# Last attention of an eleven-stage kernel: the largest scores subtracted in quarters of TensorE's rows, once a step

## The reference

```python
xq, xk, xv = jnp.split(hidden_states @ qkv_w.T + qkv_b, ...)   # 16 query heads, 4 key/value heads, D = 64
xq = xq * (1.442695041 / 8 * softplus(scaling))
scores = jnp.einsum('bqhd,bkhd->bhqk', xq, repeat(xk, 4))
probs = jax.nn.softmax(scores, axis=-1)
out = jnp.einsum('bhqk,bkhd->bqhd', probs, repeat(xv, 4))
return out.reshape(B, S, H * D) @ o_w.T + o_b
```

## Time and profile before

| | us |
|---|---|
| median of 3 runs | 2960.47 |
| lowest, highest | 2956.91, 2961.09 |
| the profiled execution | 2955.35 |
| its span, first to last instruction | 2953.2 |
| TensorE busy | 2582.3 |
| DVE busy | 2001.4 |
| ACT busy | 1426.9 |
| POOL busy | 1199.8 |

### The profile page before, as it was taken

How to read it: one execution, slowest core, us unless ns; L and a number is a source line. 1 busy time by engine, 2 the same in 40 slices (tenths; PEclk the granted TensorE clock), 3 DMA queues, 4 the chain that set the end, 5 groups by cost and what they waited for, 6 DMA issues and landing times.

```text
span 2953.2 us, 40282 instructions
## 1 busy us (share of the span) xinstructions
PE 2582.3 (87%) x15225; PEld 1239.7 (42%) x15230; DVE 2001.4 (68%) x3126; ACT 1426.9 (48%) x2454; POOL 1199.8 (41%) x677
## 2 busy tenths in 40 slices
PE   6679995897666997799868999999999999999898
PEld 4423333444223776477732333333333333333344
DVE  7676666404886775477567888778887888788502
ACT  5455552313543775377633555545554555455421
POOL 1135550000694554255411555545554555455300
PEclk9699997898787999899989999999999999999999
DMA  5000001001001000000000000000000000000000
GB/s 193 1 1 1 1 1 44 1 0 40 0 0 54 1 1 1 1 1 2 16 0 1 9 9 8 9 8 9 9 9 8 9 9 8 9 9 9 4 0 15
DMA packets 20685, 37.40 MB, mean 13 GB/s; under 512 B 10446, under 2 KB 12622, under 8 KB 19468
## 3 DMA queue, kind: packets, MB, share of 16 engines
q1 hardware_dynamic: 20492, 34.83, 3.4%
HBM read 32.47 MB, written 2.35 MB: 12 GB/s over the span
## 4 chain that ended last, share of the span: by engine, by line
PE 55%; DVE 27%; POOL 7%; issue 6%; ACT 4%; DMA 0%; ACTq 0%; DVEq 0%; POOLq 0%; SPq 0%
PE PS L2342 12%; PE PS L2333 11%; PE PS L1147 7%; DVE NR L2549 5%; PE PS L2303 4%; POOL WK L1551 4%; POOL WK L1904 4%; DVE WK L1854 2%; DVE W L2567 2%; DVE WK L808 2%; PE PS L1133 2%; ACT WK L767 1%; DVE WK L1870 1%; DVE WK L1864 1%; PE PS L2289 1%
## 5 line engine op out<-in xcount | busy, mean ns | idle before, releaser
L2549 DVE TENSOR_REDUCE NR<-PS 128x2 f32<-128x1024 f32 x512 | 626.3, 1223 | 208.4 <-PE PS L2304 208.3
L2444 ACT ACTIVATE WK<-PS 128x1024 f32<-128x1024 f32 x512 | 497.0, 1022 | 488.9 <-PE PS L2333 416.2
L2619 POOL TENSOR_TENSOR W<-W,WK 128x1024 f32<-128x1024 f32 x224 | 527.1, 2353 | 478.9 <-DVE W L2567 410.5
L2342 PE MATMUL PS<-WK,W 128*64 128x512 f32 x2048 | 494.1, 603 | 0.0
L2333 PE MATMUL PS<-WK 64*128 64x512 f16 (+1 forms) x4096 | 485.2, 377 | 0.0
L2567 DVE TENSOR_TENSOR W<-W,WK 128x1024 f32<-128x1024 f32 x224 | 284.8, 1272 | 14.7 <-ACT WK L2444 14.3
L2333 PEld LDWEIGHTS PS<-WK 64*128 64x128 f16 (+1 forms) x4096 | 199.2, 94 | 219.9 <-ACT WK L2444 6.5
L868 POOL TENSOR_TENSOR WK<-WK 128x512 f32<-128x512 f32 x128 | 166.1, 1298 | 178.1 <-ACT WK L761 178.1
L2303 PE MATMUL PS<-WK 64*128 64x512 f16 x512 | 196.5, 384 | 37.2 <-DVE NR L2549 35.0
L2342 PEld LDWEIGHTS PS<-WK,W 128*64 128x64 f32 x2048 | 124.0, 136 | 249.3 <-issue 174.3
L1147 PE MATMUL PS<-WK,W 128*128 128x512 f32 x512 | 220.1, 592 | 0.0
(11 more groups left out here) (362 smaller groups left out, 4660.7 us busy)
## 6 DMA issues: line engine op xcount, KB each, us to landing
XB<-l_rdens SPq DMA_DIRECT2D x62, 128.0 KB, 2.9
W<-in_mw SPq DMA_DIRECT2D x8, 512.0 KB, 12.1
W<-in_l2w SPq DMA_DIRECT2D x1, 3114.0 KB, 10.2
W<-in_f1w SPq DMA_DIRECT2D x1, 2816.0 KB, 18.8
W<-in_l3w SPq DMA_DIRECT2D x1, 2816.0 KB, 9.6
W<-in_f3w SPq DMA_DIRECT2D x1, 2816.0 KB, 11.2
W<-in_mw SPq DMA_DIRECT2D x8, 256.0 KB, 12.0
CBB<-in_cbb SPq DMA_DIRECT2D x1, 1360.0 KB, 8.4
```

The lines of the kernel that those rows point to most:

```text
L2342: m = e.matmul(k.PS[64 * i:64 * i + 64, 4, :], self.V[:, kt, g, :], self.PTB[kt // 2 % 2][:, kt % 2, i, :], start=kt == 0, stop=kt == NT - 1)
L2444: e.activation(self.PTB[kt // 2 % 2][:, kt % 2, :, :], self.k.PS[:, 2 * (kt % 2):2 * (kt % 2) + 2, :], ACT.Exp, scale=1.0 / 64).then_inc(s ...
L2549: e.tensor_reduce(self.PM[ji % 2][:, u // 4, :, u % 4], self.k.PS[:, 6:8, :], AX.X, ALU.max).then_inc(self.maxes.sem)
L2619: e.tensor_tensor(ac, ac, p, ALU.add).then_inc(self.acc1.sem)
```

## The change

The fourth part leaves the loop of scores. A new function, `pe_shift`, does it for both tiles of the step at once: four matmuls, each on a quarter of the rows (32 rows of `part`, now 1/32, by 32 rows of `MX`), into banks 0, 1, 2 and 3. It stands behind the first maxima of the step. Both tiles raise `score` there, one on the second and one on the fourth of these matmuls.

```diff
                 self.pe_max(e, j0, u0)
+                self.pe_shift(e, ji)
                 if g == self.PROJECT and ji + 2 < 32:
...
-        parts = ((self.KH[:, g, s_], qh), (self.KL[:, g, s_], qh), (self.KH[:, g, s_], ql), (self.part, mx))
+        parts = ((self.KH[:, g, s_], qh), (self.KL[:, g, s_], qh), (self.KH[:, g, s_], ql))
         for j, (keys, queries) in enumerate(parts):
             for i in range(2):
                 own = slice(64 * i, 64 * i + 64)
-                m = e.matmul(k.bank(2 * (kt % 2) + i), keys[own, :], queries[own, :], start=j == 0, stop=j == 3)
-        m.then_inc(self.score.sem)
+                e.matmul(k.bank(2 * (kt % 2) + i), keys[own, :], queries[own, :], start=j == 0, stop=False)
+
+    def pe_shift(self, e, ji):
+
+
+        for a in range(2):
+            for i in range(2):
+                rows = slice(64 * i + 32 * a, 64 * i + 32 * a + 32)
+                m = e.matmul(self.k.bank(2 * a + i), self.part[rows, :], self.MX[ji % 2][rows, :], start=False, stop=True)
+            m.then_inc(self.score.sem)
...
-        e.memset(self.part, 1.0 / 64).then_inc(self.const_part.sem)
+        e.memset(self.part, 1.0 / 32).then_inc(self.const_part.sem)
```

More of the change, by code:

```diff
@@ L2322, in pe_scores @@
         s_, n = slice(kt * 128, (kt + 1) * 128), 16 * ji + kt
-        qh, ql, mx = self.QH[ji % 3], self.QL[ji % 3], self.MX[ji % 2]
+        qh, ql = self.QH[ji % 3], self.QL[ji % 3]
         if not kt:
```

## The result

The changed kernel takes 2973.2 us (median of 5 runs, 2970.82 to 2974.71) against 2960.47 (2954.8 to 2961.09): the ratio is 1.0052, 95% interval 1.0041 to 1.0063. The forecast was 2976, slower by 0.55%. The profiled execution took 2971.78 us (2971.5 had been worked out for it); its span is 2969.7, 16.5 above before. The medians moved by 12.7 us and not by the 16 of the forecast.

The account below looks back on a forecast made before the run. TensorE was taken to bound the kernel (1094 of 1117 us busy), with DVE close behind. Terms 16.7 - 1.2 + 0.7 gave +16 us, so 2976 us on the median, 0.55% slower; range 2953 to 2994.

Parts of the forecast that it names:

- M1 to M0: Plain step, second maxima (M1) to first maxima (M0): 1.96 to 1.72 us; 0.24 saved, 0.19 becomes waiting for DVE.
- M0 to the weighing: Plain step, first maxima to weighing: 0.31 us to the added four matmuls, then 0.32 to the weighing, including shape changes.
- The weighing: Plain step, weighing and the second maxima behind it: stays at 1.88 us, with DVE's 3.98 us loop still covered.
- 185 plain steps: Six of eight steps in 30 full jobs, plus 5 steps of job 30: 0.09 us longer each, +16.7 us.
- Steps 5 and 6: Two steps of each job already set by DVE, at 4.28 and 4.59 us: no change.
- Steps without maxima: The 11 steps with no DVE wait: 3.70 to 3.59 us each, -1.2 us in all.
- The end: Last step, scores' start to DVE's sum: 3.14 to 3.85 us because exponentials start later, +0.7 us.
- Rival A: Entering the quarters costs nothing: plain step 4.13 us, total 2956.5, almost all within 0.2%; chance 0.22.
- B: The four matmuls run as two successive pairs, +0.22 us a step: about +68, 3028 us; chance 0.08.
- C: First maxima do not wait for DVE: step 4.04 us, -19, 2941 us; chance 0.10 including free entry with part of this.

Follow-up runs that it names:

- halved reductions: DVE reduces 256 of 512 columns of each bank: 2895.46 us (ratio 0.9795) in the changed kernel, 2919.11 us (ratio 0.988) in the kernel before.
- the first experiment: Changed kernel with the four quarter matmuls in front of the first maxima instead of behind: 2957.08 us against 2956.74 for the kernel before, ratio 1.0002.
- the halves: Changed kernel with the fourth part on 64-row halves again, as two pairs, still behind the first maxima: 2993.71 us, ratio 1.0124.
- the second pack: Changed kernel with the four quarter matmuls issued twice in a row, with 1/64, same result: 3020.84 us, ratio 1.0217.

## Why the prediction was right

Term by term, by its own steps:

1. *M1 to M0, 1.96 to 1.72.* Measured 1.953 to 1.716. The halved reductions show the cause: 0.195 of the 0.43 saved had turned into the wait.
2. *M0 to the weighing, 0.31 and 0.32.* Measured 0.322 and 0.324. This was the open term, since no row of before had a 32-row operand behind a 64-row one. The change costs 0.095 (the first experiment) or 0.096 (against the halves), as at the 8-row matmul of the earlier trace rows. The hundredth missed is the 0.01 of fill behind a pair that had waited, which the prologue's row had in its 0.32; with halved reductions, where M0 does not wait, M0 to the four is 0.312. The Trainium skill, page "TensorEngine Tiling (Array Packing)", section Tiling Modes, says that a change of the tiling mode drains TensorE; the runs agree that it costs time, 0.095 us from 64 to 32 rows, and do not show how. The prediction had worked out 0.1 us a step more from the figure of 3.07 times in the Trainium skill, page "TensorE: Matmul & The Clock Gate", section Part 3: Packing small matmuls. Inside this stream no run shows that: the second pack adds 0.216.
3. *The weighing, 1.88.* Measured 1.870; DVE's loop stayed below it.
4. *185 plain steps by 0.09, 16.7 us.* Measured 0.100 in the median step. Added up over the stage the six positions became 18.1 us longer, steps 5 and 6 1.0 shorter and the last steps 1.0 shorter, 16.1 in all. The 185 steps at 0.100 would be 18.5. Nine of them, steps 0, 1 and 3 of the three jobs in which DVE also works on the layer norm, did not change, since DVE sets them in both kernels; the forecast had counted them in (-0.9). The first step of all became 0.4 shorter, and 1.0 comes from the clock, told below.
5. *Steps 5 and 6 unchanged.* Step 6 was; step 5 went from 4.291 to 4.324. There M0 started 0.14 behind the reduction, not 0.05. That pair waits on a second signal as well, the one of the new queries. ACT had raised it by 2063.81, 1.8 before the reduction ended at 2065.61, so it was not late; whether waiting for two signals costs the 0.09 was not tested. That steps 5 and 6 became shorter in sum comes from single steps, up to 0.9 us too long, of which the trace before has six and the changed one two; they were not traced further.
6. *Steps without maxima, -0.11.* Measured -0.104.
7. *The end, +0.7.* From the last scores to POOL's last sum (2761.64 to 2766.61 before, 2776.77 to 2782.75 after) it is 1.0 us more. From the last scores to DVE's sum it is 3.89 for 3.14, 0.75 more as priced; the other quarter is that sum itself, 2.01 us for 1.76. No exponential held the scores up: with halved reductions the twelve take 1.295 to M0, six pairs of 0.216, and from the weighing to the scores it is 1.870 in the steps without maxima of both kernels.

The stage, first scores to last scores, is 16.1 longer (1164.96 to 1181.08), the end 1.0, and behind it 0.3 more, where the sum of the denominators ran at a granted clock of 0.50 and took 1.97 us for 1.08. The first scores start 1.0 earlier (1596.68 to 1595.69), which has nothing to do with the change, since one of the first stages, whose code is the same, is already as much earlier (the first matmul of L716 at 132.7 for 133.7). Together 16.4, against 16.5 of the spans. That the profiled execution came within 0.3 us of the 2971.5 is luck: the step's hundredth (+1.9 us), the clock (+1.0 in the stage, +0.3 behind it) and the end (+0.3) on one side, the nine steps (-0.9), the first step (-0.5), steps 5 and 6 (-1.0) and the earlier begin (-1.0) on the other were not forecast and nearly cancel.

The clock in the stage, which the prediction read as 1.00: in step 3 of jobs 9, 17 and 25, the three with the layer norm, TensorE waits about 2.7 us for DVE in both kernels, and in step 4 behind it the granted clock can fall to 0.50 (1.2 GHz). In the kernel before it fell in job 9, in the changed one in jobs 17 and 25. First a row of the kernel before in job 9, then one of the changed kernel in job 17, with the columns of the earlier trace rows:

```profile
1945.95:1949.30 3.35, 3.35 (x17) 1.16 (x14) 2.30 (x3) 1.63 (x2) 1.71 (x2) 0.50 0.27 73
2252.20:2255.50 3.30, 3.30 (x12) 0.71 (x8) 2.53 (x3) 1.71 (x2) 1.82 (x1) 0.50 0.22 79
```

Step 4, with its projection, takes 5.19 us before and 5.29 after at the full clock, 6.83 (before) and 6.67 and 6.52 (after) with such a stretch. Why the clock fell in one of these jobs and not in another no run shows.

Rival A failed by the 0.095 on entry, B by the second pack of 0.216, C by the 1.716.

## What to carry to other kernels

A matmul packed into quarters of the array is cheap in stream but brings its own shape; count the changes of shape in the loop before and after, not only the columns. When work moves away from between two instructions that wait on another engine, look up the shortest distance that this wait allows: here 0.43 us were taken out where only 0.24 could be used. To see whether such a wait or the work itself decides, shorten the other engine's part in both kernels: the sign of this change turned from +0.5% to -0.8%.

## What the runs showed of the hardware

Four bf16 matmuls of 32 rows by 512 columns, on four quarters of the rows and into four banks, start within 10 ns and take the same 0.216 us of stream as two of 64 rows on halves. Going from 64-row to 32-row operands costs 0.095 us, back 0.10 (the 0.327 of the first experiment less 0.216 and 0.01), and the first matmul behind a change 0.01 more; f16 to bf16 in one shape costs nothing (the eight pairs of a step before, with both types, start 0.216 apart). These hold at a granted clock of 1.00.

DVE's reduction starts 0.43 us after the pair of matmuls that it reads, and the weights that wait for its end load 0.05 after it. Here the wait of 0.2 us is visible in the distances between starts and not in TensorE's busy time.

TensorE's granted clock also fell to 0.50 in the prologue, where every pair of maxima waits for DVE. Between 1572.9 and 1583.1 us of the changed kernel it was 0.50, after waits for DVE of 0.60 to 1.08 us before each pair from 1559.9 to 1572.3, and a pair of maxima took 0.60 us for 0.39. With halved reductions it stayed at 1.00 there, in both kernels.
